# Attention: the twelfth of thirteen key steps with two maxima and no more, and one GpSimd addition that waits for VectorE's

## The reference

```
q = rms_norm(linear(layernorm(x), q_w, q_b), norm_q_w)       # (4, 512, 16, 32)
k, v = rms_norm(linear(ctx_txt, k_w, k_b)), linear(ctx_txt, v_w, v_b)
k_img, v_img = the same of ctx_img, with weights of its own
out = linear(softmax(q k^T / sqrt(32)) v + softmax(q k_img^T / sqrt(32)) v_img, o_w, o_b)
x = x + tanh(g_xattn) * out
x = x + tanh(g_ffn) * moe(layernorm(x))
```

## Time and profile before

| | |
|---|---|
| median of three runs | 1857.91 us (1856.69 to 1858.56) |
| the profiled execution's own time | 1861.8 us |
| its span, first to last instruction | 1860.5 us |
| TensorE busy | 96% of the span |
| VectorE busy | 65% |
| GpSimd busy | 51% |
| ScalarE busy | 44% |
| mean granted clock of TensorE | 0.963 |

### The profile page before, as it was taken

How to read it: one execution, slowest core, us unless ns; L and a number is a source line. 1 busy time by engine, 2 the same in 40 slices (tenths; PEclk the granted TensorE clock), 3 DMA queues, 4 the chain that set the end, 5 groups by cost and what they waited for, 6 DMA issues and landing times. The chain is left out here.

```text
span 1860.5 us, 24747 instructions
## 1 busy us (share of the span) xinstructions
PE 1779.8 (96%) x8822; PEld 1128.5 (61%) x8822; DVE 1200.9 (65%) x2242; ACT 819.4 (44%) x1517; POOL 940.5 (51%) x321
## 2 busy tenths in 40 slices
PE   5999999999999999999999999998899899999999
PEld 4888878863444445444444445432577687888777
DVE  5776676665877777877777787843554445444465
ACT  4443323344555554555455554564222155554221
POOL 3222312125776664776646777465052357767452
PEclk9999999997999999999999999996899999999999
DMA  9456759553443552453453453401141468887432
GB/s 306 152 165 198 225 165 236 167 163 105 128 120 106 134 134 57 121 134 101 125 134 72 112 128 92 118 13 68 39 147 57 142 193 262 270 268 254 157 119 91
DMA packets 185250, 268.73 MB, mean 144 GB/s; under 512 B 24972, under 2 KB 122012, under 8 KB 184612
## 3 DMA queue, kind: packets, MB, share of 16 engines
q1 hardware_dynamic: 180008, 250.36, 46.0%
q0 software_dynamic: 5120, 16.78, 2.6%
HBM read 194.10 MB, written 105.93 MB: 161 GB/s over the span
## 5 line engine op out<-in xcount | busy, mean ns | idle before, releaser
L1077 ACT ACTIVATE P<-ps 128x512 f32<-128x512 f32 (+1 forms) x832 | 442.1, 598 | 361.0 <-PE ps L952 295.1
L629 DVE TENSOR_REDUCE mp<-ps 128x1 f32<-128x448 f32 x768 | 441.3, 615 | 136.5 <-PE ps L436 132.8
L1260 POOL TENSOR_TENSOR sacc<-sacc,P 128x2048 f32<-128x2048 f32 x96 | 441.3, 4597 | 13.9 <-ACT P L1077 0.4
L436 PE MATMUL ps<-Kst,Qst 96*128 96x448 f32 (+1 forms) x1024 | 386.2, 389 | 17.0 <-DVE mp L629 16.6
L952 PE MATMUL ps<-Qst,Kst 100*128 100x512 f32 (+1 forms) x832 | 342.5, 429 | 9.4 <-ACT P L1077 9.3
L436 PEld LDWEIGHTS ps<-Kst,Qst 96*128 96x128 f32 x1024 | 197.2, 193 | 224.7 <-DVE mp L629 132.6
L907 PE MATMUL ps<-P,Vg 128*32 128x512 f32 (+2 forms) x1792 | 254.4, 644 | 6.6 <-issue 6.6
L805 POOL TENSOR_TENSOR cl<-craw,ch 128x1024 fp32r<-128x1024 f32 (+2 forms) x26 | 62.0, 2384 | 286.3 <-ACT ch L541 286.3
L952 PEld LDWEIGHTS ps<-Qst,Kst 100*128 100x128 f32 (+1 forms) x832 | 157.8, 191 | 79.4 <-ACT P L1077 54.4
L49 PE MATMUL ps<-W,ch 128*128 128x512 f32 (+1 forms) x408 | 162.5, 398 | 0.0
L51 PE MATMUL ps<-W,cl 128*128 128x512 f32 (+1 forms) x408 | 159.8, 392 | 0.0
(11 more groups left out here) (229 smaller groups left out, 3043.0 us busy)
## 6 DMA issues: line engine op xcount, KB each, us to landing
gur<-in_w_gate_up SPq DMA_DIRECT2D x23, 1024.0 KB, 7.9
Kst<-KHd SPq DMA_DIRECT2D x32, 640.0 KB, 8.0
Vd<-vf SPq DMA_DIRECT2D x50, 256.0 KB, 2.4
craw<-in_ctxT SPq DMA_DIRECT2D x24, 512.0 KB, 4.4
KHd<-sth SPq DMA_DIRECT2D x24, 512.0 KB, 3.6
KLd<-stl SPq DMA_DIRECT2D x24, 512.0 KB, 4.8
dnr<-in_w_down SPq DMA_DIRECT2D x23, 512.0 KB, 3.9
xg<-Xg SPq DMA_DIRECT2D x23, 512.0 KB, 8.0
```

What stands on the lines that cost most here:

```text
L436: pe.matmul(ps[:, bank, 0:c1 - c0], Qst[G % 3][0:96, j, 128 * qt:128 * qt + 128], Kst[G % 2][0:96, j, c0:c1], start=True, stop=True).then_ ...
L629: dve.reduce_max(out, ps[:, bank, 0:c1 - c0], AX.X).then_inc(d_ra, 1)
L1077: act.activation(P[slot(G, kt)][:m, j, :], ps[:m, 2 + (e - 1) % 3, :], ACT.Exp, scale=SCALE).then_inc(a_exp, 1)
L1260: pool.tensor_tensor(sacc[:], (P[slot(G, 0)] if kt == 1 else sacc)[:], P[slot(G, kt)][:], ALU.add).then_inc(g_sum, 1)
```

## The change

`UNITS` is changed so that all but two units of a group stand in steps 0 to 10; step 11 has two in place of six. In VectorE's step 11 the text maxima come first, then the first reciprocal, then the addition of step 8's P. And GpSimd's oi += ot waits for that addition.

```
-    UNITS = (5, 5, 4, 6, 5, 6, 5, 6, 5, 6, 5, 6, 0)
+    UNITS = (7, 6, 4, 6, 5, 6, 6, 5, 6, 5, 6, 2, 0)
...
             elif kt == 11:
-                units(G + 1, at, upto[2] - at)
+                units(G + 1, at, sum(plan))
+                if more:
+                    dve_text_maxima(G + 1, ra)
                 reciprocals(pG, (0,))
                 if G < NG:
                     dve.wait_ge(a_exp, exp_no(G, 8, 3))
                     dve.wait_ge(g_sum, sum_no(G, 7))
                     dve.tensor_tensor(sacc[:], sacc[:], P[slot(G, 8)][:], ALU.add).then_inc(d_add, 1)
-                units(G + 1, upto[2], sum(plan[2:]))
-                if more:
-                    dve_text_maxima(G + 1, ra)
...
         def normalise(G):
             ot, rt = ot2[:, G % 2, :], rt2[:, G % 2, :]
+            pool.wait_ge(d_add, G + 2)
             pool.wait_ge(d_oi, G + 1)
             pool.wait_ge(d_img, 2 * G + 2)
             pool.tensor_tensor(oi[:], oi[:], ot, ALU.add).then_inc(g_oi, 1)
```

## The result

| | before | changed |
|---|---|---|
| median, 18 runs each | 1857.81 us (1849.76 to 1862.45) | 1851.12 us (1844.10 to 1856.34) |
| ratio, 95% interval | | 0.9972 (0.9960 to 0.9985) |
| profiled execution: own time, span, clock | 1861.8, 1860.5 us, 0.963 | 1853.3, 1852.0 us, 0.972 |

The kernel is 0.3% faster, with the interval clear of one. The medians differ by 6.7 us; by the ratio it is 0.28%, 5.2 us. Of the kernel before, one slow run in the experiments' first set took 7183.55 us and counts in no ratio.

The account below looks back on a forecast made before the run. TensorE bounds the kernel, idling and slowing at group boundaries behind VectorE's maxima. Boundary gains less new key waits gave 19 us, less 8 for clock drops 11: 1850.8 us profiled, 1847 us median; range 1842 to 1855, 8 in 10 1830 to 1864.

Parts of the forecast that it names:

- The addition and GpSimd's add: Step 11: addition shrinks to 2.23 us, idle time and clock drop go, step 12's first exponential has cover.
- Four units out of step 11: Between `text_end` and the transposes: transposes, the maxima's rows and `image` come 0.9 us earlier than in an undisturbed boundary.
- The same four, ahead: Moved units cost 0 in step 0, 0.54 us until oi in step 1, 0.2 us in steps 3 to 10.
- The wait for the last key columns: Step 1: ninth unit waits 1.4 us for DMAs, groups 0 to 13; slow SP issues add 1.0 us in four.
- The undisturbed boundary: From `text_end` to the next group's first weighing without clock drop, 21.36 us in groups 5, 9, 13; forecast 22.6 us.
- The clock at the new wait: Behind the key wait in step 1: five clock drops at 1.6 us each, 8 us in all; bounds 0 and 14 drops.
- the four long waits: Key waits of 2.3 us or more in groups 4, 7, 10 and 13, where SP issues slowly; each was to bring a drop.
- Group 14: Last group, no ninth unit behind it: gains about the 4 us between a long and an undisturbed boundary.
- No drop at the new wait: Rival: the key wait in step 1 never lowers the clock, 1839 us; chance 0.15.
- Drops everywhere: Rival: the key wait lowers the clock in every group, 1861 us, or 1872 if half last long; chance 0.18.
- The keys in time: Rival: the nine DMAs land before the ninth unit needs them, so no wait in step 1, 1815 us; chance 0.12.
- That step 12's exponential waits: Rival: GpSimd's late sums hold step 12's first exponential, TensorE idles there, the drop stays, 1854 to 1862 us; chance 0.05.

Follow-up runs that it names:

- the experiments' first set: The first four of the eight follow-up kernels, measured with their own runs of the kernel before, whose median was 1853.24 us.
- the kernel with four maxima in steps 4 to 10: Changed kernel with steps 0 and 1 as before, step 11's four maxima moved to steps 4 to 10 alone: 1833.39 us, ratio 0.9890.
- the ninth unit late: Changed kernel with step 1's second-place unit moved, so that the ninth unit, which waits for the last key columns, comes behind `image_end`: 1829.08 us, ratio 0.9850.
- the kernel with the key wait early: Kernel before plus GpSimd's wait, maxima unmoved; only the wait for the last key columns moved from the ninth unit to the seventh: 1867.78 us, ratio 1.0068.
- the kernel with the old counts: Kernel before plus GpSimd's wait, six units kept in step 11, but VectorE does all maxima ahead of the addition: 1870.00 us, ratio 1.0094.

## Why the prediction was right in direction and too large in size

The forecast was 1847 us, 11 us gained; measured are 1851.12 us, 6.7 gained. The time is within the range, on the side forecast, and the mechanism was the one described. But the gain of the forecast was 0.6%, that measured 0.3%, about half of it: the step that failed is the price of the clock at the new wait, forecast 8 us, some 13 by the runs. By the prediction's own steps:

**The addition and GpSimd's add: right.** 2.23 to 2.29 us in all groups, nothing idle in step 11, no drop in step 12, and step 12's first exponential held. What I failed to draw from my own rows is that the second edit alone restores the undisturbed boundary in every group. The kernel with GpSimd's wait alone has shown it in all but two of groups 1 to 13, at 1816 us. I costed the edits as one bundle, and so took the moved maxima as part of what brings the gain.

**Four units out of step 11: 0.9 us forecast.** Measured 0.7: transposes start 564.31 - 557.77 = 6.5 us behind `text_end` in group 2, against 7.2 in the earlier trace rows. The same 0.7 in the kernel with four maxima in steps 4 to 10.

**The same four, ahead: 0.54 and 0.2 us.** 0.54 was right (6.35 - 5.81 us in the rows above). The two units in step 0, taken at 0, cost about 0.2: from `image` to `image_end` it is 574.14 - 567.04 = 7.10 us in the changed kernel and 667.44 - 660.51 = 6.93 with the old counts. The 0.2 for steps 3 to 10 was not seen, 28.33 us against 28.4, but where TensorE also projects, behind groups 4 and 12, these steps take 40.9 us against 40.45, for which the sum has no term.

**The wait for the last key columns: right in place, less in size.** I had 1.4 us in each of 14 groups and 4 for slow issues, 23.6 in all. The page has 15.2, 16.0 with group 4's, and that with three waits at the first unit of step 0 that I hadn't named. SP was slow in three groups, 7, 10 and 13, not in four. Where TensorE waits 1.06 or 1.27 us there, in groups 2 and 12, no wait on the keys is left at the ninth unit of the same group, since it comes later by as much, and so behind the landing.

**The undisturbed boundary: 22.6 us forecast, 22.6 to 22.9 measured.** The agreement is in part luck. The wait is shorter than in my sum, and the transposes are later than in it; the units in step 0 take their 0.2 us, and in seven groups `image` starts 0.1 to 0.6 us later than the 7.94 us behind `text_end` of groups 5, 9 and 13, of which the profile shows only a part as a wait for keys. With the ninth unit late it is 21.5 us, where 21.36 - 0.7 + 0.54 would be 21.2: there two maxima more stand behind `image_end`, 1.07 us, and one unit less ahead of it, 0.2.

**The clock at the new wait: the term that failed.** I had five short drops at 1.6 us, 8 in all. It was seven, five of them 6.8 us long or more, and some 13 us. I took their length from the thought that dense work follows; the kernel with the key wait early has drops of 10.2 us in just that work. I also tied drops to the four long waits, but four followed waits of 1.03 to 1.26 us. Price and number both were too low: 13 / 7 = 1.9 us a drop against 1.6, and seven against five. These 5 us are more than the forecast is off, 4.1 by the medians and 2.5 by the profiled executions (1853.3 against 1850.8). The other differences nearly cancel: the waits are 8 us less than in the sum; the later transposes, the units in step 0 and the late starts of `image` take some 7 back; of the steps behind, 3 us less are paid than forecast in the plain groups and some 1 more where TensorE projects. These sizes are estimates from one profile of each kernel.

**Group 14: 4 us forecast, 5 measured.** From group 13's `image` to group 15's, 108.1 us became 102.9. What the clock does behind the last units differs between profiles: before and two of the experiments have 27.3 us at the lower level there in one piece, GpSimd's wait alone among them, the changed kernel pieces of 3.4 and 6.8. So this is not to be put down to the change alone, and its agreement with the forecast is luck in part.

**The rivals.** No drop at the new wait: there were seven. Drops everywhere: nearer than I had it. In the kernel with the key wait alone early they stand behind twelve of thirteen waits, most of 10.2 us, and the program is slower than before by 0.7%. The keys in time: eleven waits speak against it; the kernel with the ninth unit late, where most are gone, takes 1829 us. That step 12's exponential waits: not here, but in the kernel with the old counts, 2.50 us in each group.

So of the 37 us between the kernel before and the one with GpSimd's wait alone, the change reaches 7. From group 0's `image` to group 13's (13 periods), the profiles have 720.0 us before, 715.9 changed and 686.0 with GpSimd's wait alone. Of the 30 between the last two, some 12 are the clock (group 13's wait and drop lie behind these periods) and 13.4 the waits for keys, 13.8 less the 0.4 that the other kernel has too. The remaining 4 to 5 are what the moved units cost in the boundary and in the steps with projections, less the 0.7 us for the transposes.

## What to carry to other kernels

Cost each line of a change by itself before the bundle: one wait of a GpSimd instruction whose result nobody needed yet took away the idle time and every drop between 470 and 1220 us, and the rest of the edit brought a wait of its own. When work is moved forward in a list that is numbered, look at which numbered item carries a wait and where it comes to stand; the place of one unit was worth some 20 us here. And in a program bound by TensorE, an idle time of 1 us is to be priced with the clock behind it, which here cost up to three times the wait.

## What the runs showed of the hardware

**VectorE's addition beside a GpSimd one.** 128x2048 float32 take 2.29 us alone and 3.28 when GpSimd's 128x512 addition, 1.28 us long, starts 0.14 us ahead: 1.0 us more, nearly what was left of GpSimd's. The Trainium skill's page "SBUF — State Buffer", section "SBUF: two separate sides", says that the two engines share one pair of ports and that whoever starts first has it for the whole instruction while the other blocks. By that rule the addition would be late by 1.28 - 0.14 = 1.14 us, and the trace is near it with 1.0. The kernel without GpSimd's wait shows it at other distances (VectorE, then GpSimd, group 2):

```profile
556.40 2.58 DVE L1201 TENSOR_TENSOR sacc<-sacc,P 128x2048 f32<-128x2048 f32 x1
...
555.55 1.27 POOL L1266 TENSOR_TENSOR oi<-oi,ot 128x512 f32<-128x512 f32 x1
```

Here GpSimd's add has 0.42 us left when the addition starts, and that takes 0.35 us more than its 2.23. In group 10 0.83 us are left and it takes 0.75 more, in group 6 1.00 and 0.93. So the addition loses what is left of GpSimd's, less some 0.07 us.

**The clock after short waits.** In the changed kernel idle times of 1.04 us at 520.86 and of 1.19 at 965.19 were followed by 6.8 us at 1.2 GHz, and idle times of 1.06 at 566.43 and 0.94 at 624.77 by none. With VectorE's order and the old counts a wait of 2.50 us in each group was followed by the lower level in most, but not in groups 1 and 3; this is group 3:

```profile
615.00:619.00 4.00, 4.00 (x35) 0.73 (x33) 3.40 (x5) 1.82 (x4) 0.16 (x1) 1.00 0.09 18
```

So the length of an idle time alone doesn't tell whether the clock falls. The Trainium skill's page "TensorE: Matmul & The Clock Gate", section "Why this matters for your kernels", asks for gaps no longer than about 3 us. The trace doesn't agree that shorter ones are safe.

**What a drop costs.** 10.2 us at the lower level cost 3.6 us behind the wait of the kernel with the key wait alone early, 6.8 us 1.6 to 1.9 behind the ninth unit of the changed kernel, but 3.2 us in step 12 before. Why the same length costs less behind the ninth unit no run shows; that VectorE's maxima pace TensorE there in part, so that a slower matmul is in part covered, is my guess.
